# A fused attention and mixture stage on one core: its loop over node groups written out, with constant waits and addresses

## The reference, cut to what matters

```python
h = jnp.einsum('ni,hio->hno', x, W)                       # 8 heads of 32
edge_attn = leaky_relu(attn_src[:, src] + attn_dst[:, dst], negative_slope=0.2)
edge_attn_exp = jnp.exp(edge_attn - jnp.max(edge_attn))
attn_norm = edge_attn_exp / (segment_sum(edge_attn_exp.T, dst)[dst].T + 1e-10)
x = x + segment_sum(attn_norm[..., None] * h[:, src], dst) + _layernorm(x)
...
w = softmax(feat @ Wr + br)                               # weights of 8 experts
h = relu(_bn(einsum(feat, W1) + b1)); h = relu(_bn(einsum(h, W2) + b2))
y = einsum(h, Wo) + bo
x = x + sum over experts e of w[:, e] * y[:, e]
```

## Time and profile before

| what | value |
|---|---|
| median of 3 runs | 6731.94 us (6723.11 to 6738.67) |
| the profiled execution: its span, from the first to the last instruction (no time around it is given) | 7570.3 us |
| PE, DVE, ACT, POOL busy in that span | 71%, 55%, 23%, 54% |
| `attend_mix` in that span | about 430 to 3970 us |

### The profile page before, as it was taken

The page is one execution under the profiler, slowest core; times in us unless marked ns, Lnnn a source line. Parts: engine busy times, 40 slices in busy tenths (PEclk is TensorE's granted clock), DMA queues, the critical chain, the costliest instruction groups (busy, mean ns, idle before and its releaser), DMA issues. The chain is left out here.

```text
span 7570.3 us, 107731 instructions
## 1 busy us (share of the span) xinstructions
PE 5337.8 (71%) x32067; PEld 4729.9 (62%) x32068; DVE 4174.6 (55%) x9813; ACT 1761.8 (23%) x4052; POOL 4078.1 (54%) x4039
## 2 busy tenths in 40 slices
PE   5249989999899898999994555544554456454887
PEld 4248888888888888888883434333433344343887
DVE  6347778777787787777772233222332223232676
ACT  3103333333333333333340000000000000000554
POOL 1455555555565655555534666655665666663111
PEclk9568999999999999999996777766776777776999
DMA  7454444554454454544533333333333333332221
GB/s 211 127 145 122 128 129 131 133 136 127 128 134 130 130 131 124 138 125 132 136 92 93 107 114 106 112 99 101 104 114 97 98 103 101 101 105 86 84 76 49
DMA packets 639191, 878.18 MB, mean 116 GB/s; under 512 B 254782, under 2 KB 447376, under 8 KB 638050
## 3 DMA queue, kind: packets, MB, share of 16 engines
q0 software_dynamic: 183392, 501.66, 24.5%
q1 hardware_dynamic: 424972, 334.16, 15.5%
q10 hardware_dynamic: 30326, 35.87, 1.4%
HBM read 766.70 MB, written 155.49 MB: 122 GB/s over the span
## 5 line engine op out<-in xcount | busy, mean ns | idle before, releaser
L1241 POOL DMA_INDIRECT m_ring<-tab_a,m_src x1764 | 1912.8, 1084 | 1354.6 <-DMA m_dstb<-dst_p 783.8
L1883 POOL DMA_INDIRECT eb_rows<-tab_b,eb_src x1764 | 1750.6, 992 | 581.7 <-issue 536.4
L2124 PE MATMUL eb_acc<-eb_rows,eb_S 128*128 128x257 f32 x3528 | 1041.8, 451 | 281.9 <-issue 277.2
L2124 PEld LDWEIGHTS eb_acc<-eb_rows,eb_S 128*128 128x128 f32 x3528 | 802.7, 231 | 477.6 <-issue 339.7
L1539 PE MATMUL m_acc<-m_V,m_S 128*128 128x264 f32 x3528 | 909.3, 402 | 23.0 <-issue 20.7
L1539 PEld LDWEIGHTS m_acc<-m_V,m_S 128*128 128x128 f32 x3528 | 668.8, 199 | 145.9 <-issue 48.7
L1667 ACT ACTIVATE mh_high<-m_ps,bn_b,bn_s 128x256 fp32r<-128x256 f32 x784 | 441.5, 563 | 1156.6 <-remote 601.8
L521 DVE TENSOR_TENSOR mh_low<-mh_full,mh_high 128x512 fp32r<-128x512 f32 x784 | 542.9, 693 | 129.1 <-ACT mh_full L1667 99.1
L1654 ACT ACTIVATE mh_full<-m_ps,bn_b,bn_s 128x256 f32<-128x256 f32 x784 | 400.6, 564 | 895.5 <-DVE mh_low L521 348.3
L1324 DVE TENSOR_TENSOR m_V<-m_ring,m_V 128x1280 f32<-128x1280 f32 (+1 forms) x392 | 532.7, 1359 | 58.1 <-DVE m_V L1321 0.5
L1524 PEld LDWEIGHTS m_psE<-q,m_ST 128*128 128x128 f32 x3528 | 458.3, 199 | 127.3 <-issue 121.7
(11 more groups left out here) (367 smaller groups left out, 10751.7 us busy)
## 6 DMA issues: line engine op xcount, KB each, us to landing
m_dstb<-dst_p SPq DMA_DIRECT2D x196, 320.0 KB
m_dstb<-dst_p SPq DMA_DIRECT2D x196, 256.0 KB
buf<-empty SPq DMA_DIRECT2D x49, 771.0 KB
m_ring<-tab_a,m_src POOLq DMA_INDIRECT x1764
eb_rows<-tab_b,eb_src POOLq DMA_INDIRECT x1764
xw_stage<-in_L_ffn_w_dram ACTq DMA_DIRECT2D x16, 1024.0 KB
over<-b_blank SPq DMA_DIRECT2D x9, 1452.0 KB
mOV<-over SPq DMA_DIRECT2D x49, 264.0 KB
```

The lines of the kernel that those rows point to most:

```text
L1241: gp.indirect_dma_start(out=ring[:, j, :], out_offset=None, in_=scratch["tab_a"], in_offset=bass.IndirectOffsetOnAxis(ap=src[:, j:j + 1], ...
L1883: gp.indirect_dma_start(out=rows_[q.par][j][:, t, 0:D], out_offset=None, in_=scratch["tab_b"], in_offset=bass.IndirectOffsetOnAxis(ap=src_ ...
L2124: last_i = nc.tensor.matmul(ps_acc[j][:, 0:NR], S[q.par][j][:, t, :], rows_[q.par][j][:, t, :], start=t == 0, stop=t == WT - 1)
```

## The change

All 49 groups are written out in program order, with no loop. Group numbers are then Python integers, so every wait is for a constant, the register work goes, and so do all calls of `hold` in this stage.

```diff
-        self.exists = not isinstance(q.n, int) or 0 <= self.a < 4 * NT
+        self.exists = 0 <= self.a < 4 * NT
...
-    passed, filled = map(s_, ("passed", "filled"))
+    filled = s_("filled")
...
     def groups(eng, body):
 
-        body(Group(0, 0, 0), False, True)
-        with eng.Fori(0, (Q - 5) // 2) as i:
-            body(Group(i * 2 + 1, i, 1), True, True)
-            body(Group(i * 2 + 2, i + 1, 0), True, True)
-        for n in range(Q - 4, Q):
-            body(Group(n, n // 2, n % 2), True, n < Q - 1)
+        for n in range(Q):
+            body(Group(n, n // 2, n % 2), n > 0, n < Q - 1)
...
                 at_least(sp, V_ok, s.a - 3)
-                hold(sp, passed)
                 at_least(sp, ST_ok, s.a - 1)
-                hold(sp, passed)
...
                 v.wait_ge(f_ok, s.a + 1)
                 at_least(v, summed, s.a - 1)
-                hold(v, passed)
                 to = V[s.side]
                 nc.vector.tensor_tensor(to[:, 0:size, D:NA], f[:, 0:size, 0:H], f[:, 0:size, H:2 * H], MAX).then_inc(w_ok, 1)
                 v.wait_ge(w_ok, s.a + 1)
-                hold(v, passed)
...
-                nc.vector.tensor_tensor(den[p][:, :, :], U[:, :, D:NA], corr[:, bass.ds(q.n * GM, GM), :], ADD)\
+                nc.vector.tensor_tensor(den[p][:, :, :], U[:, :, D:NA], corr[:, q.n * GM:q.n * GM + GM, :], ADD)\
...
                 pe.wait_ge(ST_ok, s.a + 1)
                 at_least(pe, f_ok, s.a - 1)
-                hold(pe, passed)
                 for j in range(s.size):
                     last_i = nc.tensor.matmul(psE[s.side][:, j * 16:j * 16 + 2 * H], ST[s.side][:, j, :],
-                                              k["q"][:, bass.ds(s.n, 1), :].rearrange("p x c -> p (x c)"), start=True, stop=True)
+                                              k["q"][:, s.n, :], start=True, stop=True)
```

More of the change, by code:

```diff
@@ L1206, in body @@
                         store(q.prev(), q.n * 2 + 1)
-                    if e == 4 and after and not (isinstance(q.n, int) and q.n + 2 >= Q):
+                    if e == 4 and after and q.n + 2 < Q:
                         load(q.next().next())
@@ L1238, in gather @@
                 gp.wait_ge(staged[s.c], s.n * 48 + 48)
-                hold(gp, passed)
                 for j in range(s.first, s.first + s.size):
@@ L1644, in copy_sum @@
                 at_least(s, x1_ok, q.n)
-                hold(s, passed)
                 nc.scalar.copy(U[:, j, :], ps_acc[at.par][:, 0:NA]).then_inc(U_ok, 1)
```

## The result

The changed kernel takes **6532.29 us** in the median of 4 runs (6529.53 to 6535.86), the kernel before 6734.99 us (6723.11 to 6738.67): a ratio of 0.9697, with an interval of 0.9679 to 0.9716, or 203 us less. The forecast was 6637 us. The direction was right, the size less than half, and the time lies at the low edge of the range.

A forecast was written before the change was run, and what follows sets the result against it. The prediction took PE to bound the stage, waiting little more than 2 us a group, mostly for DVE's small gaps. 81 us from DVE plus 14 from PE's loop end made 95 us off 6731.94: 6637 us, range 6530 to 6735.

The forecast's parts named there:

- DVE's helpers and register work: DVE's waits for its own last instruction shrink to 34 ns, cutting PE's waits: 1.65 us a group, 81 us (0 to 120).
- The loop's end on PE: PE's branch between groups goes; mostly hidden, 0.67 us idle at each of 21: 14 us, between 0 and 77.
- The Trainium skill's rule: By it alone for all PE branches the loop's end would be 77 us; DVE's 63 ns branch disagreed, so 14 was taken.
- Helpers of PE, ACT, POOL and SP at nothing: PE's helpers hidden by matmuls handed out ahead, the others' by idle time; removing them was priced at nothing.
- The stretches at 0.72 us: Stretches in nearly every group with a PE matmul every 0.72 us, 374 us in all, judged to belong to the profiled execution.
- the 63 to 65: Estimated length in us of a timed group of the stage, from two groups without the slow stretch.
- 61.7 us: PE's work in a group, taken to be nearly all of the time after the change.
- 2.45: PE's average wait in us a group, read from two groups; all of it going would give 120 us.
- The larger gain: Rival: slow PE stretches are in timed runs too and fed by helpers; a quarter going adds 93 us: 6544 us, chance 0.22.
- The 6535 us: Another way to the larger gain: all PE waits of 120 us go, with the branch at its bound of 77.
- DVE's time did not become idle time: Rival: DVE's saved time becomes its idle time, only the loop's end counts: 14 us, 6718 us, chance 0.14.
- The straight program does not arrive late: Rival: written-out groups make PE or DVE wait for instruction fetches, 179 us for one a group: 6816 us, chance 0.16.

The follow-up runs named there:

- e12: Kernel before with 12 of DVE's 13 kinds of helper gone, loop and register work kept on all engines: 6643.15 us.
- e7: Changed kernel with the helpers back on DVE alone, no loop on any engine: 6566.24 us.
- e1: Kernel before with all 49 groups written out with constant waits on all engines, every helper kept: 6582.57 us.
- e6: Kernel before with four groups in the loop's body on every engine, eleven turns in place of 22, helpers and register work kept: 6653.23 us.
- e9: Changed kernel with DVE alone back in its loop, with its helpers and register work: 6652.36 us.
- e10: Changed kernel with PE alone back in its loop, with its helpers: 6603.13 us.
- e2: Kernel before with only DVE's groups written out and only DVE's helpers gone; the other engines loop with helpers: 6604.34 us.
- e5: The kernel before, unchanged, profiled once more: 6726.56 us.
- e8: Changed kernel with the helpers back on PE alone, no loop on any engine: 6530.00 us.
- e11: Changed kernel with ACT, POOL and SP back in their loop with helpers; DVE and PE written out without helpers: 6536.96 us.
- e4: Kernel before with ACT, POOL and SP written out without helpers; PE and DVE loop with helpers: 6709.98 us.

## Why the prediction was right in direction and too small

- **DVE's helpers and register work (81 us).** The mechanism was right: the gaps fell to 34 ns as forecast. The size depends on what else is there. With the loop left in place 12 of the 13 kinds of DVE's helpers measured 82 us (e12), in the straight program 34, and all helpers 50 (e7, e1). That 82 is so near 81 is partly luck: PE's waits fell by 47 us in e12 (81.6 + 19.4 to 54.0, from 700 to 3300 us), and the 81 counted waits of PE alone, and register work as well, which e12 keeps.
- **"The loop's end on PE" (14 us, bounded by 77).** This step failed. The loop measured 148 us when it goes first (e1; e6 gives 147), and 203 - 82 = 121 us are left for it, the register work and the other engines' helpers when DVE's helpers go first (e12). There are three reasons. DVE's end was taken to cost nothing, by the length of its branch in the earlier trace rows; the stop comes behind the branch, in the idle time before the first instruction of the next turn, a row that I had not read (66.8 us of "issue" before L1289 in the trace of before too). With DVE's helpers in place it is worth 86 us (e9). PE's part measured 73 us (e10), five times the 14: its idle time was taken from one end, 0.67 us, where e2 gives 1.7 and e10 1.9 us on average (40.3 / 21). And it was left out that PE's clock falls behind many of these stops; the 0.94 of the earlier trace rows was a sign of a lower clock, though in that execution also of its slow stretches (0.98 in e5).
- **The Trainium skill's rule** ("Runtime: NRT & Kernel Launch", section "Instruction fetch mechanics": a taken branch to code that is no longer held waits for its fetch, and kernels prefer full unrolling where possible) was set aside because DVE's row seemed to speak against it. Read at the right place the trace agrees, with 5.64 us on PE and 3.0 us on DVE, and with a transfer of instructions in each of the stops (e5, e9, e10).
- **Helpers of PE, ACT, POOL and SP at nothing:** right (e8, e11). But ACT's, POOL's and SP's, or their interplay with DVE's, may hold the 16 us that e1 has over e7 and e8.
- **The stretches at 0.72 us as a thing of one execution:** right (e5). The timed group is 64.3 us on average in e5, within the 63 to 65. But PE's work in it is not 61.7 us: without stops and at the full clock a group takes 60.6 to 60.8, so that there were 3.6 us a group to gain and not 2.45.
- **Rivals.** The larger gain came, not by the stretches. The 6535 us that the prediction gives by another way is 3 us from the result, but by luck in the parts: it had 120 us of waits for DVE's gaps and 77 of PE's branch, where helpers cost 50 to 82 and the loop's end 121 to 148, over half of it on DVE where e9 and e10 put it back alone. DVE's time did not become idle time without use: PE lost all waits. The straight program does not arrive late: 3.92 and 1.76 MB of instructions in place of the earlier trace rows, and no wait of PE from 609.5 to 3398.2 us.

## What to carry to other kernels

Price a loop's end by the idle time of the first instruction behind the branch, on every engine, and by the rate of the products that follow; the branch's own record shows neither. Ask whether a transfer of instructions runs in that idle time. A stop on the second-busiest engine can cost nearly its whole length, but not in every kernel: PE waited for DVE's stops where DVE had its helpers and PE no loop of its own (e9), and for none where it was the other way round (e12). Write out the engines that stop: PE and DVE alone gave all of it here (e11, 6537 us).

## What was not expected of the hardware

- The same loop ends cost ACT, POOL and SP next to nothing: the next instruction comes 0.18 to 0.21 us behind the branch (turns of 187, 113 and 257 recorded instructions), on ACT also with 371 (e6). SP with 510 stands still for 3.7 us, DVE with 337 or 441 for 2.9 to 3.9 (medians of the kernels), while a DVE turn of 95 in an earlier phase goes on after 0.23 us.
- PE's branch is longer where DVE turns in a loop too: 5.6 us with all engines (e5), 5.9 with PE and DVE (e4), 5.3 in e12, against 4.8 when PE alone loops (e10) and 4.6 with all but DVE (e2). Why was not tried.
- A stop of 2.1 us on PE was followed by about 7 us at the lower clock and, on top of the stop, by a group that was 3.1 us longer (e10).
